# Cross-attention, attention and expert kernel: expert chunks stored and loaded one tile earlier, turned rows for two value projections from a second area, two buffers for finished values

## The chip, the cores and the metric

The kernel runs on one core of a Trainium2 chip. The metric is the device time of one execution in microseconds (us). The median of three runs of the kernel before is 1504.02 us (1499.2 to 1504.85).

## What is computed

Two layers in float32 over x of 8 batches, 512 tokens and 512 features, each behind a layer norm and added to its input. The first is a cross-attention in which every token looks at itself and at 77 context rows. The second adds a self-attention with 16 heads and a mixture of 8 experts, two of them per token.

```python
def xattn(h, ctx):                       # h = layernorm(x)
    q, k_tok, v_tok = h @ Wq + bq, h @ Wk + bk, h @ Wv + bv
    k_ext, v_ext = ctx @ Wk + bk, ctx @ Wv + bv
    scores = concat([sum(q * k_tok, -1)[..., None], einsum('bsh,beh->bse', q, k_ext)], -1)
    p = softmax(scores)
    return p[..., :1] * v_tok + einsum('bse,beh->bsh', p[..., 1:], v_ext)

def ffn(h):                              # h = layernorm(x1)
    q, k, v = split(h @ W_qkv + b_qkv)   # 16 heads of 32
    attn_out = softmax(q @ k.T / sqrt(32)) @ v
    top_g, top_i = top_k(softmax(h @ W_gate + b_gate), 2)
    moe_out = sum over the 2 chosen experts of g * (h @ W_experts[e] + b_experts[e])
    return attn_out + moe_out

x1 = x + xattn(layernorm(x), ctx)
out = x1 + ffn(layernorm(x1))
```

## The kernel before

Five programs, one for each engine queue, are written by hand and meet at semaphores; no scheduler moves anything. TensorE (PE) multiplies, VectorE (DVE), ScalarE (ACT) and GpSimd (POOL) do the elementwise work, and SyncE (SP) issues nearly all DMAs, in the order of its program. A wait in SP's program holds everything that is written behind it. Every operand of a large product is kept as a high and a low part, so that one product is three matmuls (`prod3`, lines 222 to 224).

The program has four stages.

- **Setup** (to about 118 us) prepares the folded weights.
- **Tile stage** (about 118 to 450 us). 32 tiles of 128 tokens (`NT` = 32, four in a batch, `T` = 4) go through the cross-attention, the second norm and the gate. Each engine has a `steps(b, part)` that lists its work of one tile step with an offset: ACT's step i does `p_hi` of tile i-1 (L704), `chunk_hi` of chunk i (L698), `weigh` of tile i (the softmax's exponential, L709), `h_hi` of i+1, `h_norm` of i+2, `h2_hi` of i-2, and `h2_norm` of tile i-1 (L660). DVE's step i begins with `p_lo` of i-1 (L1251), and has `largest` of i (to L1274), `x1_whole` of i-1 (L1280), `share` of i (L1286, L1288), `h2_stats`, `h_lo` (L1245) and at its end `chunk_lo` (L1303). PE's step ends with `p_turn` of tile i (L947), which needs `share`. POOL computes the two norms' factors (L516 to L522). Beside the tiles, each step splits one chunk of the expert weights (128 x 512, 32 chunks in all) into a high and a low part: SP loads it to one of two staging buffers `raw` (`load_chunk`, L358), ACT and DVE write the parts to one of two buffers `chunk`, and SP stores them (`store_chunk`, L362).
- **Attention stage** (about 487 to 1222 us). 8 batches of 16 heads. While batch b's heads run, the dense products of the later heads (items R0 to R3) and of batch b+1 (V0 to V3 for values, N0 to N3 for queries and keys) are cut in halves and laid between them by the tables `HALVES` and `STEP`: R3 at head 4, V0 begins at head 5, V1 ends at head 7, V2 begins at head 13. All products read the turned rows of the batch, `fT`, four tiles of 128 x 1024, which SP fetches from DRAM (`fetch_turned`, L355) once R3 is done with the previous contents. `V` is copied from `Vst` by a DMA at the batch's start (L441). The `L415` DMAs stack query and key rows. DVE's `finish` divides a pair of heads by its sums and writes it to `tmp` (L1567); after four pairs POOL adds `tmp` to the output in DRAM (`attended`, L548), twice in a batch (h = 0 and 1). The first pair of each half waits until the addition before has landed (`f_att_out`).
- **Expert stage** (to the end). 72 blocks of 128 chosen rows are gathered (L590), turned, multiplied with an expert and added to the output (L601).

Of the kernel before, what the change touches and what calls it, by code (L numbers as in the profile page):

```python
# [6 lines left out]
ALU = mybir.AluOpType  # L7
# [8 lines left out]
def program(nc, x, ctx, wq, bq, wk, bk, wv, bv, w_qkv, b_qkv, w_gate, b_gate, w_exp, b_exp, out):  # L16
# [15 lines left out]
    C = D // P  # L32
# [12 lines left out]
    with ExitStack() as stack:  # L45
# [26 lines left out]
        def full(part):  # L72
            return part.bitcast(F32)
# [54 lines left out]
        fT = (fT_all[:, :, 0], fT_all[:, :, 1])  # L128
        fT_in = full(area(parts, 6 * C * D, T, 2 * D))
        NSLOT = 5  # L130
        SLOTS = (r0, r0 + 4 * S, r4, r4 + 4 * S, r4 + 8 * S)
# [15 lines left out]
        Osb = area(plain, p1, QW)  # L147
        tmp = area(plain, p1 + S, T, D // 2)
        bvf = sb("bias_v_all", [P, D])
# [46 lines left out]
        p2 += NE * D  # L196
        rows = [area(plain, p2 + D * i, D) for i in range(4)]
        ysb = [area(plain, p2 + D * (4 + i), D) for i in range(4)]
        col = sb("col", [P, 2, 4])
# [9 lines left out]
        in_list in_be r_ranked ws_in0 ws_in1 ws_hi ws_lo ws_out0 ws_out1 m_ready in_ew0 in_ew1 in_ew2 in_ew3 in_ew4 in_ew5 in_ew6 in_ew7 m_rows0 m_rows1  # L209
        m_rows2 m_rows3 m_tr m_hi m_hT m_full m_sum m_y m_added0 m_added1 m_added2 m_added3 m_done f_att_out x1_out0 x1_out1 x1_out2 x1_out3  # L210
        h2_out0 h2_out1 h2T_out0 h2T_out1 h2T_out2 h2T_out3 made_gate made_steps""".split()
# [124 lines left out]
        def _(sp):  # L336
# [28 lines left out]
            def tiles(b, more, first=False):  # L365
                for t in range(T):
                    if t or not first:
                        store_chunk(b + (t - 1) // T, (t - 1) % T)
                    if t and (more or t < T - 1):
                        load_chunk(b + (t + 1) // T, (t + 1) % T)  # L370
                    elif not first and t == 0:
                        load_chunk(b, 1)
                    if not more and t == 2:

                        sp.wait_ge(q["v_full"], NT)
                        for u in range(T):
                            sp.wait_ge(q[f"h2T_out{u}"], 16)
                        fetch_turned(0)
                    if more:

                        sp.wait_ge(q["x1_part"], b * T + t + 1)
                        sp.dma_start(xin[:, t, :], x_t[b * T + t + T]).then_inc(q[f"x_in{t}"], 16)
                    sp.wait_ge(q["x1_ready"], b * T + t + 1)
                    sp.dma_start(out_t[b * T + t], x1[:, t, :]).then_inc(q[f"x1_out{t}"], 16)
                    sp.wait_ge(q["h2_ready"], b * T + t + 1)
                    sp.dma_start(h2_t[b * T + t], h2[:, t % 2, :]).then_inc(q[f"h2_out{t % 2}"], 16)
                    if t or not first:
                        turned_out(b * T + t - 1, t + T - 1)
# [7 lines left out]
            tiles(B - 1, False)  # L396
            store_chunk(NE - 1, C - 1)
            turned_out(NT - 1, T - 1)
# [29 lines left out]
            def load_expert(r):  # L428
# [6 lines left out]
                sp.dma_start(ew[r], ws_dram[bass.ds(e, 1)].rearrange("e p n -> p (e n)")).then_inc(q[f"in_ew{r}"], 16)  # L435

            def batch(b, first, last):
                sp.wait_ge(q["f_d_free"], number(b, "R0")[0])
                sp.sem_inc(q["sp_went_on"], 1)
                await_ge(sp, "f_pv", 2 * b * NQ)  # L440
# [49 lines left out]
        def _(pool):  # L490
# [53 lines left out]
            def attended(b, h):  # L544

                pool.wait_ge(q["f_o_fin"], b * NQ + 4 * h + 4)
                pool.sem_inc(q["pool_went_on"], 1)
                pool.dma_start(out_b[b][:, :, h * (D // 2):(h + 1) * (D // 2)], tmp, accum_op=ALU.add).then_inc(q["f_att_out"], 16)  # L548

# [59 lines left out]

            pool.wait_ge(q["f_att_out"], 16 * 2 * B)  # L610
            for i in range(NB):
# [228 lines left out]
        def _(pe):  # L840
# [146 lines left out]
            def dense(b, item, n, o, half=""):  # L987
                kind, t = item[0], int(item[1])
                cs = {"": range(C), "a": range(C // 2), "b": range(C // 2, C)}[half]
                if kind == "V":  # L990
                    if half != "b":
                        pe.wait_ge(q[f"f_in{t}"], b * 16 + 16)
                    for c in cs:
                        last = prod3(pe, o[:], at(fT, sl, t, c), at(wV, sl, c), c == 0, c == C - 1)
                else:
# [172 lines left out]
        def _(dve):  # L1168
# [326 lines left out]

            big = area(plain, 3 * C * D + T * D + NT * NE, NB, NE)
            other = area(plain, 3 * C * D + T * D + NT * NE + NB * NE, NB, NE)

# [57 lines left out]
            def finish(b, p):  # L1556
# [6 lines left out]
                if p % HG == 0:  # L1563
                    await_ge(dve, "f_att_out", (2 * b + p // HG) * 16)
                for m in range(2):
                    at_d = m * P + p % HG * HD
                    ins = dve.tensor_tensor(  # L1567
                        tmp[:, :, at_d:at_d + HD].rearrange("p (x t) d -> p t x d", x=2),
                        bank[6][:, 0:QW].rearrange("p (t m x d) -> p m t x d", t=2, m=2, x=2)[:, m],
# [38 lines left out]
            def blocks(n, part):  # L1608
                for k in range(U):
# [6 lines left out]

                    await_ge(dve, "m_done", i - 3)
                    dve.tensor_tensor(ysb[k % 4], bank[2 + k % 2][:], be_all[:, bass.ds(e * D, D)], ALU.add).then_inc(q["m_sum"], 1)  # L1618

# [33 lines left out]
```

## Time and profile before

| | |
|---|---|
| runs | 1499.2, 1504.02, 1504.85 us; median 1504.02 |
| profiled execution | 1503.07 us, of which the span (first to last instruction) is 1501.4 us |
| PE | 1351.7 us busy, 90% of the span; mean granted clock 0.935 |
| DVE | 968.8 us, 65% |
| ACT | 902.2 us, 60% |
| POOL | 358.6 us, 24% |
| SP's DMA queue | 166.13 MB, 37.3% of the 16 DMA engines' time |
| POOL's DMA queue | 42.04 MB, 16.5% |

An engine's busy share is an average over stages with different limits, so the stages are read apart. PE's matmuls are pipelined and their ends are modelled. A wait is put down to the releaser that came last. In a line of the timeline the number in brackets is the idle time of the engine before that instruction and the arrow names what ended it. The granted clock is a share of full speed.

### The profile page before, as it was taken

What the parts mean: (1) busy time and instruction counts of PE and PEld (TensorE: products, weight loads), DVE (VectorE), ACT (ScalarE), POOL (GpSimd) and SP (SyncE); (2) the same over time, 40 slices, a digit from 0 to 9 for tenths busy, and PEclk for the clock granted to TensorE, in tenths of its full rate; (3) what the DMA queues carried; (4) which work ended last, traced back from release to release, by engine and by line L of the source; (5) the groups of instructions that cost most, each with busy time, mean ns of one, the idle gap of its engine ahead of it and who ended that gap; (6) DMA issues with size and microseconds to landing.
All of it is one profiled execution on the core that took longest, in us unless ns stands there. A gap on an engine that the chain in (4) does not pass through costs nothing. (4 is left out here: it accounts for less than half of the span.)

```text
span 1501.4 us, 27639 instructions
## 1 busy us (share of the span) xinstructions
PE 1351.7 (90%) x7744; PEld 1028.0 (68%) x7745; DVE 968.8 (65%) x2143; ACT 902.2 (60%) x1888; POOL 358.6 (24%) x572
## 2 busy tenths in 40 slices
PE   4989989898988889999999999999997769999997
PEld 4957777776777556676676767667774437777775
DVE  4246666666666888787887878888885633433332
ACT  4123333333334778899999989999996753333332
POOL 0001112121110001121211112120001007777765
PEclk9998887989899999999999999999997779999998
DMA  5014555555557523646445474544567757877873
GB/s 153 1 58 161 201 191 194 197 197 194 200 180 221 148 58 94 155 99 159 86 100 136 107 154 98 141 91 111 132 115 185 278 196 137 145 130 126 146 128 57
DMA packets 111371, 212.49 MB, mean 142 GB/s; under 512 B 28265, under 2 KB 36585, under 8 KB 109139
## 3 DMA queue, kind: packets, MB, share of 16 engines
q1 hardware_dynamic: 82048, 166.13, 37.3%
q0 software_dynamic: 26624, 42.04, 16.5%
q10 hardware_dynamic: 2643, 3.65, 0.8%
q8 instruction: 27, 0.44, 0.1%
q14 instruction: 29, 0.24, 0.1%
HBM read 79.48 MB, written 77.73 MB: 105 GB/s over the span
## 5 line engine op out<-in xcount | busy, mean ns | idle before, releaser
L222 PE MATMUL banks<-parts 128*128 128x512 f32 (+6 forms) x1108 | 453.8, 410 | 57.4 <-DVE parts L1245 19.6
L224 PE MATMUL banks<-parts 128*128 128x512 f32 (+6 forms) x1108 | 432.0, 390 | 0.0
L223 PE MATMUL banks<-parts 128*128 128x512 f32 (+6 forms) x1108 | 431.7, 390 | 0.0
L1538 DVE TENSOR_REDUCE plain<-banks 128x1 f32<-128x512 f32 x512 | 339.6, 687 | 95.6 <-PE banks L1042 89.6
L766 ACT ACTIVATE banks<-banks,plain 128x512 f32<-128x512 f32 x512 | 345.0, 678 | 14.9 <-DVE plain L1538 14.6
L773 ACT ACTIVATE plain<-banks 128x1024 f32<-128x1024 f32 x256 | 265.7, 1038 | 60.5 <-PE banks L1064 58.9
L222 PEld LDWEIGHTS banks<-parts 128*128 128x128 f32 (+1 forms) x1108 | 220.8, 199 | 114.9 <-issue 46.9
L224 PEld LDWEIGHTS banks<-parts 128*128 128x128 f32 (+1 forms) x1108 | 219.8, 198 | 41.7
L223 PEld LDWEIGHTS banks<-parts 128*128 128x128 f32 (+1 forms) x1108 | 221.4, 200 | 30.6
L1042 PE MATMUL banks<-parts 96*128 96x512 f32 x512 | 186.5, 417 | 0.7 <-ACT banks L766 0.3
L1064 PE MATMUL banks<-parts 104*128 104x512 f32 x512 | 180.7, 435 | 6.0 <-ACT plain L773 4.6
L548 POOL DMA_DIRECT2D out_dram<-plain x16 | 22.2, 1390 | 575.0 <-DVE plain L1567 490.8
L816 ACT CAST parts<-banks 128x512 fp32r<-128x512 f32 x72 | 42.1, 586 | 170.6 <-PE banks L1140 170.6
L1618 DVE TENSOR_TENSOR plain<-banks,plain 128x512 f32<-128x512 f32 x72 | 49.8, 692 | 142.5 <-PE banks L224 127.5
L1083 PE MATMUL banks<-plain,parts 128*32 128x256 f32 x2048 | 132.2, 401 | 0.2 <-ACT plain L773 0.2
L698 ACT CAST parts<-plain 128x512 fp32r<-128x512 f32 x32 | 19.9, 620 | 181.5 <-DMA plain<-in_L_ffn_W_experts_dram 181.5
L601 POOL DMA_INDIRECT out_dram<-plain,score_bias x72 | 114.0, 1583 | 53.0 <-issue 24.6
L1042 PEld LDWEIGHTS banks<-parts 96*128 96x128 f32 x512 | 99.3, 195 | 38.6 <-issue 8.8
L766 ACT ACTIVATION_READ_ACCUMULATOR banks<-banks,plain 128x1 f32 x512 | 115.1, 225 | 0.0
L1064 PEld LDWEIGHTS banks<-parts 104*128 104x128 f32 x512 | 86.6, 196 | 33.2 <-issue 15.0
L1083 PEld LDWEIGHTS banks<-plain,parts 128*32 128x32 f32 x2048 | 62.2, 114 | 63.3 <-issue 32.1
L516 POOL TENSOR_TENSOR mo<-mo,consts 128x1 f32<-128x1 f32 x64 | 12.1, 190 | 377.8 <-DVE mo L1236 377.8
(180 smaller groups left out, 1602.0 us busy)
## 6 DMA issues: line engine op xcount, KB each, us to landing
parts<-parts SPq DMA_DIRECT2D x384, 128.0 KB, 2.4
experts_split<-parts SPq DMA_DIRECT2D x32, 512.0 KB, 4.3
h_turned<-parts SPq DMA_DIRECT2D x32, 512.0 KB, 2.9
parts<-h_turned SPq DMA_DIRECT2D x32, 512.0 KB, 6.8
parts<-experts_split SPq DMA_DIRECT2D x8, 2048.0 KB, 11.5
plain<-in_x_dram SPq DMA_DIRECT2D x32, 256.0 KB, 4.2
plain<-in_L_ffn_W_experts_dram SPq DMA_DIRECT2D x32, 256.0 KB, 4.3
out_dram<-plain SPq DMA_DIRECT2D x32, 256.0 KB, 2.6
```

The costliest lines, as they stand in the source:

```text
L222: pe.matmul(out, stat[0], mov[0], start=first, stop=False)
L223: pe.matmul(out, stat[0], mov[1], start=False, stop=False)
L224: return pe.matmul(out, stat[1], mov[0], start=False, stop=last)
L601: pool.indirect_dma_start(out=out_rows, out_offset=bass.IndirectOffsetOnAxis(ap=lst[:, i, 0:1].bitcast(U32), axis=0), in_=ysb[i % 4], in_o ...
L766: act.activation(bank[SB[t]][:], bank[SB[t]][:], ACT.Exp, bias=nmx[:, k, t:t + 1], accum_out=Z[:, t, k:k + 1]).then_inc(q["f_exp"], 1)
L773: act.activation(PT[k % HG][:, c:c + 2, :], banks[0][:], ACT.Exp).then_inc(q["f_pt"], 1)
L816: act.copy(gT[k][:, 0].rearrange("p c n -> p (c n)"), bank[k][:]).then_inc(q["m_hi"], 1)
L1042: pe.matmul(bank[SB[t]][:], stk[slot][0][0:M0, m, t * P:(t + 1) * P], stk[slot][1][0:M0, m, :], start=True, stop=True).then_inc(q["f_s_ful ...
L1064: pe.matmul(bank[c % 2][:], stk[slot][1][0:M1, m, c * P:(c + 1) * P], stk[slot][0][0:M1, m, :], start=True, stop=True).then_inc(q["f_t_ful ...
L1083: last = pe.matmul(bank[6][o * HD:(o + 1) * HD, 0:QW], V[:, c, head * HD:(head + 1) * HD], PT[(2 * p + m) % HG][:, c, x * QW:(x + 1) * QW] ...
L1538: dve.tensor_reduce(nmx[:, k, t:t + 1], bank[SB[t]][:], AX.X, ALU.max, negate=True).then_inc(q["f_max"], 1)
L1618: dve.tensor_tensor(ysb[k % 4], bank[2 + k % 2][:], be_all[:, bass.ds(e * D, D)], ALU.add).then_inc(q["m_sum"], 1)
```

## The change

Four edits, and some areas of on-chip memory that move.

1. **Chunks.** In SP's tile step t, `store_chunk` now takes the chunk of this tile where it took the one of the tile before, and `load_chunk` fetches the chunk of tile t+2 where it fetched that of t+1. ACT's and DVE's steps are as before.
2. **Turned rows for V0 and V1.** A new area `fU` of two tiles is filled by SP at the start of each batch but the last (`fetch_ahead`). The halves of V0 and V1 that are laid between heads read `fU`; V2, V3 and N0 to N3 read `fT`. `fetch_turned` still fetches all four tiles. The first `fetch_ahead` waits for the stored expert chunks, since `fU` lies over one of their buffers.
3. **Finished values.** `tmp` has two buffers, one for each half of a batch, and `f_att_out` becomes two semaphores. `finish` waits for the addition of the same half of the batch before.
4. **Areas.** `rows` and `ysb` of the expert stage and two temporaries of the routing move. Two of the `ysb` buffers lie over the new `tmp`, so DVE's first block waits for `f_att_out0`.

```diff
+        fU_in = full(area(parts, r4 + 12 * S, 2, 2 * D))
+        fU_all = area(parts, r4 + 12 * S, 2, 2 * D).rearrange("p t (a c n) -> p t a c n", a=2, c=C)
+        fU = (fU_all[:, :, 0], fU_all[:, :, 1])
...
-        tmp = area(plain, p1 + S, T, D // 2)
+        tmp = (area(plain, HG * T * S + D, T, D // 2), area(plain, p1 + S, T, D // 2))
...
-        rows = [area(plain, p2 + D * i, D) for i in range(4)]
-        ysb = [area(plain, p2 + D * (4 + i), D) for i in range(4)]
+        rows = [area(plain, p2 + D * i, D) for i in (0, 3, 4, 5)]
+        ysb = [area(plain, p2 + D * i, D) for i in (6, 7, 1, 2)]
...
             def tiles(b, more, first=False):
                 for t in range(T):
-                    if t or not first:
-                        store_chunk(b + (t - 1) // T, (t - 1) % T)
-                    if t and (more or t < T - 1):
-                        load_chunk(b + (t + 1) // T, (t + 1) % T)
-                    elif not first and t == 0:
-                        load_chunk(b, 1)
+                    store_chunk(b, t)
+                    if more or t < T - 2:
+                        load_chunk(b + (t + 2) // T, (t + 2) % T)
...
+            def fetch_ahead(b):
+                for t in range(2):
+                    sp.dma_start(fU_in[:, t], ft_dram[b * T + t]).then_inc(q[f"f_u{t}"], 16)
+
             def batch(b, first, last):
                 sp.wait_ge(q["f_d_free"], number(b, "R0")[0])
+                if first:
+                    sp.wait_ge(q["ws_out0"], 16 * NE * C // 2)
+                if not last:
+                    fetch_ahead(b + 1)
...
-                pool.dma_start(out_b[b][...], tmp, accum_op=ALU.add).then_inc(q["f_att_out"], 16)
+                pool.dma_start(out_b[b][...], tmp[h], accum_op=ALU.add).then_inc(q[f"f_att_out{h}"], 16)
...
                 if kind == "V":
-                    if half != "b":
+                    ahead = half != "" and t < 2
+                    if ahead and half == "a":
+                        pe.wait_ge(q[f"f_u{t}"], b * 16)
+                    elif half != "b":
                         pe.wait_ge(q[f"f_in{t}"], b * 16 + 16)
                     for c in cs:
-                        last = prod3(pe, o[:], at(fT, sl, t, c), at(wV, sl, c), c == 0, c == C - 1)
+                        last = prod3(pe, o[:], at(fU if ahead else fT, sl, t, c), at(wV, sl, c), c == 0, c == C - 1)
...
                 if p % HG == 0:
-                    await_ge(dve, "f_att_out", (2 * b + p // HG) * 16)
+                    await_ge(dve, f"f_att_out{p // HG}", b * 16)
...
+                    if part == "first" and k == 0:
+                        dve.wait_ge(q["f_att_out0"], 16 * B)
```

The diff moves instructions of SP alone. The first place is SP's loop of the tile stage, where its first tile step ends and its second begins. `experts_split` is the store of a chunk, `in_L_ffn_W_experts_dram` a load, `h_turned` the store of turned rows. Before:

```order
L386 DMA h_rows<-plain 128x512 [waits h2_ready]
L351 ISA [waits h2T_ready]
L351 DMA h_turned<-parts 128x1024
L362 ISA [waits ws_lo]
L362 DMA experts_split<-parts 256x1x512
L358 ISA
L358 DMA plain<-in_L_ffn_W_experts_dram 128x512
L381 REGISTER_ALU
L382 ISA [waits x1_part]
L382 DMA plain<-in_x_dram 128x512
```

Now:

```order
L386 DMA h_rows<-plain 128x512 [waits h2_ready]
L354 ISA [waits h2T_ready]
L354 DMA h_turned<-parts 128x1024
L364 REGISTER_ALU
L365 ISA [waits ws_lo]
L365 DMA experts_split<-parts 256x1x512
L361 ISA
L361 DMA plain<-in_L_ffn_W_experts_dram 128x512
L382 ISA [waits x1_part]
L382 DMA plain<-in_x_dram 128x512
```

The row order is the same; what differs is the number waited for in `ws_lo` and the chunk that is loaded, each one further on.

The second place is SP's queue at the start of the first attention batch, up to the fetch of the turned rows. Before:

```order
L415 DMA parts<-parts 32x2x512 x5
L441 DMA parts<-plain 128x2048 [waits f_d_free]
L415 DMA parts<-parts 32x2x512 [waits f_d_free,f_t_full]
L415 DMA parts<-parts 32x2x512 x5
L355 DMA parts<-h_turned 128x1024 [waits f_d_full]
L355 DMA parts<-h_turned 128x1024 x3
```

Now:

```order
L414 DMA parts<-parts 32x2x512 x5
L438 DMA parts<-h_turned 128x1024 [waits ws_out0,f_d_free]
L438 DMA parts<-h_turned 128x1024
L448 DMA parts<-plain 128x2048
L414 DMA parts<-parts 32x2x512 [waits f_d_free,f_t_full]
L414 DMA parts<-parts 32x2x512 x5
L358 DMA parts<-h_turned 128x1024 [waits f_d_full]
L358 DMA parts<-h_turned 128x1024 x3
```

Two loads of turned rows stand ahead of the copy of V; the four behind them stay.

## Rows read from the trace of the kernel before

**Rows 1.** The page, 40 equal slices of 37.5 us: granted TensorE clock in tenths.

```profile
PEclk9998887989899999999999999999997779999998
```

**Rows 2.** Windows: stretch, length, busy time (count) of PE, PEld, DVE, ACT, POOL, clock.

```profile
150.00:300.00 150.00, 133.55 (x695) 112.50 (x694) 96.68 (x284) 51.91 (x119) 28.00 (x109) 0.86 0.56 196
700.00:1000.00 300.00, 290.44 (x1896) 207.51 (x1896) 241.76 (x502) 275.72 (x597) 52.40 (x80) 0.99 0.51 120
```

**Rows 3.** Waits from 150 to 450 us: engine, line, releaser, us in total, times, longest.

```profile
ACT parts L698 <- DMA plain<-in_L_ffn_W_experts_dram: 162.4, 28, 7.2
...
PE banks L222 <- DVE parts L1245: 16.5, 17, 1.2
PE banks L947 <- DVE sc L1288: 13.7, 12, 2.2
```

**Rows 4.** Timeline, one tile step on SP and ACT: start, duration, instruction.

```profile
229.04 0.48 SPq L358 DMA_DIRECT2D plain<-in_L_ffn_W_experts_dram  x1
...
239.90 0.55 SPq L358 DMA_DIRECT2D plain<-in_L_ffn_W_experts_dram  x1
...
233.53 0.62 ACT L698 CAST parts<-plain 128x512 fp32r<-128x512 f32 x1 [6.33 <-DMA plain<-in_L_ffn_W_experts_dram]
...
237.23 0.82 ACT L660 ACTIVATE plain<-plain,mo 128x512 f32<-128x512 f32 x1 [1.08 <-POOL mo L522]
```

**Rows 5.** Line 947, the turn of the shares, once a tile; durations in ns.

```profile
L947 PE MATMUL banks<-ident,sc x32: 270/274/284, 120.4 to 448.6; 128*78 128x128 f32 x32
```

**Rows 6.** Timeline of PE: two pairs of neighbours.

```profile
173.42 0.28 PE L947 MATMUL banks<-ident,sc 128*78 128x128 f32 x1
...
181.59 0.27 PE L947 MATMUL banks<-ident,sc 128*78 128x128 f32 x1
...
224.13 0.28 PE L947 MATMUL banks<-ident,sc 128*78 128x128 f32 x1 [1.19 <-DVE sc L1288]
225.59 0.47 PE L222 MATMUL banks<-parts 128*128 128x512 f32 x1 [1.18 <-DVE parts L1245]
```

**Rows 7.** Windows of the tile stage: a step at full clock, and the stretch behind it.

```profile
214.00:222.00 8.00, 7.63 (x50) 6.56 (x49) 5.62 (x16) 1.16 (x3) 2.03 (x8) 1.00 0.63 210
225.00:235.00 10.00, 9.41 (x38) 8.37 (x39) 6.12 (x18) 2.84 (x9) 1.99 (x8) 0.59 0.61 210
```

**Rows 8.** Timeline of ACT and DVE around one step's border.

```profile
204.67 0.82 ACT L660 ACTIVATE plain<-plain,mo 128x512 f32<-128x512 f32 x1 [0.81 <-POOL mo L522]
206.42 0.26 ACT L704 CAST parts<-banks 78x128 fp32r<-78x128 f32 x1 [0.94 <-PE banks L947]
...
201.99 0.16 DVE L1286 RECIPROCAL col<-col 128x1 f32<-128x1 f32 x1 [0.96 <-ACT sc L709]
...
210.20 0.68 DVE L1280 TENSOR_TENSOR plain<-banks,plain 128x512 f32<-128x512 f32 x1
```

**Rows 9.** Waits of PE's weight loads for turned rows, 480 to 1222 us.

```profile
PEld banks L222 <- DMA parts<-h_turned: 10.6, 5, 3.3
```

**Rows 10.** Timeline of POOL: the second addition of batches 0, 5 and 6.

```profile
599.71 1.40 POOL L548 DMA_DIRECT2D out_dram<-plain  x1 [6.78 <-DVE plain L1567]
...
1041.43 1.40 POOL L548 DMA_DIRECT2D out_dram<-plain  x1 [25.59 <-DVE plain L1567]
...
1127.27 1.28 POOL L548 DMA_DIRECT2D out_dram<-plain  x1 [42.13 <-issue]
```

**Rows 11.** Batch 3: the copy of V is issued, and PE's first load that uses it.

```profile
767.37 0.53 SPq L441 DMA_DIRECT2D parts<-plain  x1
...
778.55 0.37 PEld L1083 LDWEIGHTS banks<-plain,parts 128*32 128x32 f32 x12 [0.36 <-issue]
```

**Rows 12.** Issue to landing, us, shortest, median, longest: line 355's fetches, then line 548's additions.

```profile
DMA to landing us min/median/max: 3.4/6.8/11.2
...
DMA to landing us min/median/max: 7.4/8.0/14.3
```

**Rows 13.** Timeline of DVE in batch 7: the finished values' first pair.

```profile
1141.71 0.49 DVE L1567 TENSOR_TENSOR plain<-banks,plain 128x128 f32<-128x128 f32 x2 [6.67 <-DMA out_dram<-plain]
```

More of the change, by code:

```diff
@@ L209, in program @@
         in_list in_be r_ranked ws_in0 ws_in1 ws_hi ws_lo ws_out0 ws_out1 m_ready in_ew0 in_ew1 in_ew2 in_ew3 in_ew4 in_ew5 in_ew6 in_ew7 m_rows0 m_rows1
-        m_rows2 m_rows3 m_tr m_hi m_hT m_full m_sum m_y m_added0 m_added1 m_added2 m_added3 m_done f_att_out x1_out0 x1_out1 x1_out2 x1_out3
+        m_rows2 m_rows3 m_tr m_hi m_hT m_full m_sum m_y m_added0 m_added1 m_added2 m_added3 m_done f_att_out0 f_att_out1 f_u0 f_u1 x1_out0 x1_out1 x1_out2 x1_out3
         h2_out0 h2_out1 h2T_out0 h2T_out1 h2T_out2 h2T_out3 made_gate made_steps""".split()
@@ L396, in _ @@
             tiles(B - 1, False)
-            store_chunk(NE - 1, C - 1)
             turned_out(NT - 1, T - 1)
@@ L547, in attended @@
                 pool.sem_inc(q["pool_went_on"], 1)
-                pool.dma_start(out_b[b][:, :, h * (D // 2):(h + 1) * (D // 2)], tmp, accum_op=ALU.add).then_inc(q["f_att_out"], 16)
+                pool.dma_start(out_b[b][:, :, h * (D // 2):(h + 1) * (D // 2)], tmp[h], accum_op=ALU.add).then_inc(q[f"f_att_out{h}"], 16)
             for t in range(T):
@@ L608, in _ @@
             attended(B - 1, 1)
-            pool.wait_ge(q["f_att_out"], 16 * 2 * B)
+            for h in range(2):
+                pool.wait_ge(q[f"f_att_out{h}"], 16 * B)
             for i in range(NB):
@@ L1494, in second_records @@
                 choice_records(1)
-            big = area(plain, 3 * C * D + T * D + NT * NE, NB, NE)
-            other = area(plain, 3 * C * D + T * D + NT * NE + NB * NE, NB, NE)
+            big = area(plain, 3 * C * D + T * D + 4 * NT * NE + D, NB, NE)
+            other = area(plain, 3 * C * D + T * D + 4 * NT * NE + D + NB * NE, NB, NE)
             def block_experts():
@@ L1567, in finish @@
                     ins = dve.tensor_tensor(
-                        tmp[:, :, at_d:at_d + HD].rearrange("p (x t) d -> p t x d", x=2),
+                        tmp[p // HG][:, :, at_d:at_d + HD].rearrange("p (x t) d -> p t x d", x=2),
                         bank[6][:, 0:QW].rearrange("p (t m x d) -> p m t x d", t=2, m=2, x=2)[:, m],
```

## The prediction

> **What bounds the kernel now.** I read the slices of the page first, then windows, then the waits of each window, then the timeline of single steps. The slices show three regions: a clock of 7 to 9 tenths in slices 4 to 12 (the tile stage), 9 tenths or more up to slice 30 (attention), and 7 tenths in slices 31 to 33 (the end of attention) [rows 1]. In the tile stage PE is busy 133.55 of 150 us at a mean granted clock of 0.86; in the middle of the attention stage 290.44 of 300 us at 0.99 [rows 2]. So attention is bound by PE, with little to win, while the tile stage has both idle PE and a slower clock.
>
> Who holds the tile stage? ACT waits 162.4 us, in 28 of 28 tiles, for the load of the expert chunk [rows 3]. ACT is not the busy engine (51.91 of 150 us, [rows 2]), so this costs only if it closes a circle, and it does. SP issues a chunk's load at 229.04; ACT takes the chunk at 233.53, 4.49 later; only behind it stand the softmax's exponential and the rest of ACT's step, whose last piece `h2_norm` ends at 237.23 + 0.82 = 238.05, 4.52 later; SP, whose program has the store of that row ahead of the next chunk, issues the next load at 239.90, 1.85 later [rows 4]. The sum is 10.86 us. The stage's own period: the turn of the shares runs from 120.4 to 448.6 in 31 steps [rows 5], 328.2 / 31 = 10.59 us. They agree: the tile stage runs at the pace of a circle that goes through a load issued one tile too late. All other engines fit themselves into it.
>
> **Part 1, the chunks.** The load of chunk t+2 now goes out at the place in SP's queue where that of t+1 went. Nothing is added: as many loads and stores, in the same order. SP's new wait is for the chunk that DVE has just split at the end of the step, ahead of DVE's `x1_begun`, for which SP waits next anyway; behind it are the x load and three stores, all of which wait for later pieces of DVE's program. So the wait holds nobody, and I cost it at nothing; if that cover were gone, x rows for three tiles on would be late. A load then has one whole step more than its 4.49 us, so ACT's wait of about 5.8 us (162.4 / 28) goes and the circle is open.
>
> What is late next? (a) PE. Its quickest step at full clock, without a wait, took 181.59 - 173.42 = 8.17 us [rows 6]; the mean busy time of a step is 133.55 x 10.59 / 150 = 9.43 us at clock 0.86 [rows 2], and 9.43 x 0.86 = 8.1 at full clock. Steps with the gate's products are longer than those without, so I take 8.5, the upper side. (b) The circle of ACT, DVE and POOL that stays: from `p_hi` (206.42) to the end of `x1_whole` (210.20 + 0.68 = 210.88) 4.46 us, and from `share` (201.99, the step before) to the end of `h2_norm` (204.67 + 0.82 = 205.49) 3.50 us [rows 8]; behind it `p_hi` can start again: 7.96 us. DVE alone is busy 96.68 x 10.59 / 150 = 6.8 us in a step [rows 2]. So PE binds by a small margin, at 8.5 us. The gain is (10.59 - 8.5) x 31 = **65 us**. Its bounds: at 8.1 us it is 77, and if the clock stays at 0.86 a step cannot be under 9.43, which leaves (10.59 - 9.43) x 31 = 36.
>
> **The clock** decides between these. PE waited 1.19 and 1.18 us at 224.13 and 225.59 [rows 6]; in the 8 us before the granted clock was 1.00, in the 10 us behind it 0.59, mostly the 1.2 GHz level [rows 7]. In the attention stage, with PE 97% busy, it is 0.99 [rows 2]. The tile stage's falls stand behind such gaps, and the gaps are waits for `share` and `h_lo` (13.7 and 16.5 us in [rows 3]), both of which come late because ACT waited for the chunk. With them gone I take the clock to stay at 2.4 GHz nearly throughout. The Trainium skill, "TensorE: Matmul & The Clock Gate", section "A second HAM failure mode: psum-queue depth-cycling", says that short idle spots between groups of matmuls, if frequent, are enough to make the clock swing. By that rule the clock would still swing in a step that keeps some tenths of idle time, and the gain would be the 36 us above; this trace speaks against it, as the step from 214 to 222 us kept 0.37 us idle at 1.00 [rows 7].
>
> **Part 2, turned rows ahead.** PE waited 10.6 us in five batches for the first value tile's fetch [rows 9]. `fU` is filled from the batch's start, five heads ahead, so the wait goes. What it cost in all is seen in the period: from batch 0's second addition to batch 5's 441.72 us, 88.34 for a batch, against 1127.27 - 1041.43 = 85.84 for batch 6, which had no wait [rows 10]: 5 x 2.5 = 12.5 us. That is more than 10.6, since the clock fell behind the longest wait. I take **13**; bounds 9 (ACT, busy 275.72 of 300 us, becomes the bound for a part) and 16 (the sixth batch's addition was itself issued a little late). It adds 14 fetches of 512 KB. They stand ahead of the copy of V and of the stacks for the second half. The copy of V is issued 11.2 us before PE first needs it [rows 11], and SP reaches the new fetches before it, since the copy also waits for the last products with the old V. A fetch lands in 3.4 to 11.2 us [rows 12]. I cost them at 0, at most 3 us a batch where V is pushed past its 11.2. The Trainium skill, "DMA: Bandwidth & Descriptors", section "Queues, rings and completion order", says that each DMA engine takes the descriptors of one ring in their order, so 1 MB put ahead of V must delay it by its own length if both are pending at once. By that the cost would be up to the 3 us above; no row here shows such a pair.
>
> **Part 3, two buffers.** Of 16 additions one was waited for: batch 7's first pair of finished values stood 6.67 us for the addition issued at 1127.27 [rows 13, 10], which took 14.3 us to land where the median is 8.0 [rows 12]. It now writes the other buffer, whose addition went out half a batch earlier. PE stood too, and slices 31 to 33 show a lower clock behind it [rows 1]. I take **7**; bounds 5 and 10. The extra wait of DVE's first expert block is for an addition issued some 40 us before, so it costs 0. The moved areas change no instruction: 0.
>
> **Sum.** 65 + 13 + 7 = 85 us off the profiled execution's 1503.07: 1418.07. That execution is 0.95 below the median of the runs (1504.02), so the forecast is **1418** us, 5.7% less.
>
> **Rivals.**
> - *The clock keeps swinging in the tile stage.* 36 + 13 + 7 = 56: 1447. For it: PE's margin over the circle of 7.96 is small, so waits remain; against it: [rows 7]. 0.15.
> - *Another circle binds at 9.2 us.* The circle of 7.96 passes four engines, and each landing or queue that slips adds to it; x rows must land one and a half steps ahead, with traffic denser by 10.59 / 8.5. The gain is 1.39 x 31 = 43: 43 + 20 = 63, 1440. 0.12.
> - *The change doesn't do what it says*: SP reaches the loads so late that ACT still waits, the tile stage keeps its pace and only parts 2 and 3 pay: 20 us, 1483. Against it: SP's place in the queue is unchanged and the chunk is needed a step later. 0.03.
> - *Slower.* The 1 MB ahead of V in seven batches delays V and the stacks, PE stands in each, and the clock falls. To lose 85 + 7.5 us it must cost 13 us in each batch, so V would land 24 us after its issue. The worst landings are 11.2 and 14.3 [rows 12]; the latter would cost 3.1 us a batch, 22 in all. Below 24 us this does not decide. 0.02.
> - *More than forecast*: steps of 8.1 us and all upper bounds, 77 + 16 + 10 = 103: 1400. 0.04.
>
> **How the numbers follow.** The forecast has 0.64; its own range is 1404 to 1432. The range from 1400 to 1456 takes in the two rivals at 1440 and 1447 with the cost of 3 us a batch on part of the batches, and holds some 0.9. A difference of about 0.5% (7.5 us) is what a measurement of this kernel can tell from no change. Only the fourth rival is slower; no change would need it to cost as much as the three parts give. Faster 0.96, same 0.02, slower 0.02.
>
> **What the profile after would show.** Right: no wait of ACT for chunks, line 947's 31 steps in some 263 us, PEclk 9 or full in the tile stage's slices, PE's idle time there under 0.5 us a step; no wait for the turned rows at heads 5 to 7 and batches of 85 to 86 us; no wait of DVE for an addition in batch 7. Wrong: steps of 9.4 us with PE busy at 0.86 (the clock), steps of 9 us and more with PE idle before `p_turn` or the next score (another circle, named by the releaser), ACT's wait kept, or PE waiting for V at head 3. The sum would be most wrong if the clock's falls have a cause other than PE's gaps.

## The result, and the profile after

The changed kernel takes 1406.47 us (median of four runs, 1402.42 to 1412.21), the kernel before in the same comparison 1502.62. The ratio is 0.9365, with an interval of 0.9322 to 0.9407: 6.4% less, where 5.7% was forecast (1418, range 1400 to 1456). The profiled execution of after took 1412.21 us with a span of 1410.6, against 1501.4.

The page of after, the slices of 35.3 us each, PE's busy share above and the granted clock below, to be laid beside [rows 1]:

```profile
PE   4998999999888899999999999999988779999996
PEclk9998999999899999999999999999996789999998
```

Inside the tile stage (now slices 5 to 10) the clock reads 9 throughout, and 8 in the two slices at its borders (4 and 11), where [rows 1] had 8 in five slices and 7 in one; slices 31 to 33 are as low as before. A window of 200 us in the tile stage (columns as in [rows 2]), and one of the attention stage:

```profile
130.00:330.00 200.00, 199.47 (x1234) 172.37 (x1232) 172.73 (x512) 95.20 (x212) 53.17 (x200) 1.00 0.74 259
...
700.00:900.00 200.00, 198.00 (x1321) 142.19 (x1321) 167.67 (x349) 189.71 (x412) 38.70 (x59) 1.00 0.60 143
```

PE is busy 199.47 of 200 us at full clock, against 133.55 of 150 at 0.86. It is now what bounds the tile stage. The turn of the shares, which answers to [rows 5] (line 947 is line 955 now), and the costliest waits from 130 to 380 us, which answer to [rows 3]:

```profile
L955 PE MATMUL banks<-ident,sc x32: 270/270/272, 120.7 to 371.8; 128*78 128x128 f32 x32
```

```profile
POOL mo L523 <- DVE mo L1247: 176.6, 59, 6.8
ACT sc L717 <- DVE col L1285: 93.3, 30, 4.1
ACT plain L668 <- POOL mo L529: 32.9, 30, 2.0
DVE parts L1262 <- ACT parts L712: 23.8, 29, 1.2
...
PE banks L225 <- DVE parts L1262: 2.6, 2, 1.4
```

31 steps take 371.8 - 120.7 = 251.1 us, 8.10 a step, where they took 328.2, 10.59 a step. ACT's wait of 162.4 us for the chunks has left the list; ACT now waits for DVE instead, which costs nothing, since PE waits 2.6 us for line 1262 and 0.5 us for line 1256 in the whole stretch.

One thing is new. The timeline of PE behind the last tile, then two windows there:

```profile
380.92 0.76 PE L225 MATMUL banks<-parts 128*128 128x512 f32 x1 [5.41 <-DMA parts<-h_turned]
```

```profile
372.00:382.00 10.00, 3.41 (x19) 2.63 (x19) 5.88 (x8) 4.22 (x6) 4.62 (x7) 0.84 0.88 299
382.00:392.00 10.00, 10.00 (x41) 7.95 (x40) 2.27 (x4) 3.30 (x5) 0.00 (x0) 0.82 0.45 174
```

PE stands 5.41 us for the first fetch of turned rows (line 358), and in the 10 us behind it the clock is 0.82. Before the change PE waited 0.50 us for this fetch, but it also had a wait for DVE at this border, which is 1.2 us now:

```profile
452.18 0.77 PE L222 MATMUL banks<-parts 78*128 78x512 f32 x1 [3.30 <-DVE parts L1251]
```

POOL's additions cut the attention stage, as in [rows 10] (line 548 is line 555 now): the second ones of batches 0, 6 and 7.

```profile
526.29 1.41 POOL L555 DMA_DIRECT2D out_dram<-plain  x1 [6.95 <-DVE plain L1578]
...
1039.75 1.28 POOL L555 DMA_DIRECT2D out_dram<-plain  x1 [42.06 <-issue]
...
1132.08 1.30 POOL L555 DMA_DIRECT2D out_dram<-plain  x1 [41.86 <-PE banks L1151]
```

By such marks the profiled spans divide as follows (us; the difference of the spans is -90.8):

| stretch | before | after | difference |
|---|---|---|---|
| start to the first turn of shares | 120.4 | 120.7 | +0.3 |
| 31 tile steps | 328.2 | 251.1 | -77.1 |
| last turn of shares to batch 0's second addition | 151.1 | 154.5 | +3.4 |
| batches 1 to 6 | 527.6 | 513.5 | -14.1 |
| batch 7 | 95.9 | 92.3 | -3.6 |
| to the end | 278.2 | 278.5 | +0.3 |

### The profile page after: what moved, and what is told of

It is laid out like the page before. It is cut to its first block and busy times, and to the rows that moved or that the text cites. A ratio compares the mean times of both kernels' runs of the same rounds, so it can differ in the third digit from the quotient of the medians.

```text
span 1410.6 us, 27655 instructions
## 1 busy us (share of the span) xinstructions
PE 1305.5 (93%) x7744; PEld 994.7 (71%) x7745; DVE 967.5 (69%) x2143; ACT 903.4 (64%) x1888; POOL 363.8 (26%) x572
## 5 line engine op out<-in xcount | busy, mean ns | idle before, releaser
L225 PE MATMUL banks<-parts 128*128 128x512 f32 (+6 forms) x1108 | 443.0, 400 | 32.7 <-DVE parts L1334 7.4
L227 PE MATMUL banks<-parts 128*128 128x512 f32 (+6 forms) x1108 | 423.5, 382 | 0.0
L226 PE MATMUL banks<-parts 128*128 128x512 f32 (+6 forms) x1108 | 422.9, 382 | 0.0
L225 PEld LDWEIGHTS banks<-parts 128*128 128x128 f32 (+1 forms) x1108 | 214.2, 193 | 85.4 <-issue 24.2
L227 PEld LDWEIGHTS banks<-parts 128*128 128x128 f32 (+1 forms) x1108 | 213.0, 192 | 40.8
L226 PEld LDWEIGHTS banks<-parts 128*128 128x128 f32 (+1 forms) x1108 | 214.4, 194 | 30.8
L1563 DVE TENSOR_TENSOR parts<-banks,plain 8x512 fp32r<-8x512 f32 x128 | 89.2, 697 | 21.5 <-PE banks L1064 18.0
```

Source lines behind the costliest of these rows:

```text
L225: pe.matmul(out, stat[0], mov[0], start=first, stop=False)
L226: pe.matmul(out, stat[0], mov[1], start=False, stop=False)
L227: return pe.matmul(out, stat[1], mov[0], start=False, stop=last)
L1563: dve.tensor_tensor(stk[slot][0][M0:M1, m, :].rearrange("p (t n) -> p t n", t=T), bank[6][M0:M1, 0:P].unsqueeze(1).broadcast_to([2 * T, T, ...
```

## The experiments

The first three do one part of the change each, without the others.

**The chunks alone**: edit 1.

```diff
-                    if t or not first:
-                        store_chunk(b + (t - 1) // T, (t - 1) % T)
...
+                    store_chunk(b, t)
+                    if more or t < T - 2:
+                        load_chunk(b + (t + 2) // T, (t + 2) % T)
```

> The kernel before with part 1 alone: each tile step stores its own chunk and loads the chunk two on. Theory (the tile stage ran at the pace of a circle through a load issued one tile too late; opened, PE sets the pace at its full clock): line of the turned shares at 8.1 us a step as in the changed kernel, against 10.59; 77 us less in the tile stage, of which 3 to 5 us come back where PE waits for the fetch of the first turned rows; in all 1502.6 - 73 = about 1430 us, and the clock full through the tile stage. Rival (the three parts need each other, for instance the clock stays up only together): steps of 8.5 us or more and over 1445 us.

1425.31 against 1504.57 us, ratio 0.9474 (0.946 to 0.9488): -79.3 us. The row of its turn of the shares:

```profile
L943 PE MATMUL banks<-ident,sc x32: 270/270/272, 119.4 to 369.0; 128*78 128x128 f32 x32
```

That is 249.6 / 31 = 8.05 us a step. Part 1 alone gives the full pace of the tile stage, and also the late fetch: PE waits 5.5 us there too, so that wait belongs to part 1 and not to the added fetches. In the attention stage PE's and its weight loads' waits for turned rows stay (8.6 and 10.8 us), and DVE still waits 6.4 us for an addition in batch 7.

**The second area of turned rows alone**: edit 2.

```diff
+            def fetch_ahead(b):
+                for t in range(2):
+                    sp.dma_start(fU_in[:, t], ft_dram[b * T + t]).then_inc(q[f"f_u{t}"], 16)
```

> The kernel before with part 2 alone: V0 and V1 read turned rows fetched a batch ahead. Theory: the five waits (10.6 us) go, and the clock's falls behind them; batches 1 to 5 take 85.5 us each as in the changed kernel (441.7 before, 427.8 after): 14 us less, about 1489 us, ratio 0.991. Rival (the wait was covered by ACT, busy 92% of the attention stage, and the batch got shorter for another reason, such as the two buffers): 5 us less or nothing, ratio 0.997 or more.

1491.47 us, ratio 0.9913 (0.9898 to 0.9927): -13.1 us. Its additions that end batches 0 and 5:

```profile
606.02 1.40 POOL L559 DMA_DIRECT2D out_dram<-plain  x1 [6.89 <-DVE plain L1581]
...
1033.99 1.40 POOL L559 DMA_DIRECT2D out_dram<-plain  x1 [25.59 <-DVE plain L1581]
```

Five batches take 427.97 us, 85.6 each, where they took 88.34. In the kernel after it is 427.76. No wait for turned rows is left in its attention stage. The mechanism of part 2 holds, and its size.

**Two buffers for finished values alone**: edit 3 and the areas it needs.

```diff
-                    await_ge(dve, "f_att_out", (2 * b + p // HG) * 16)
+                    await_ge(dve, f"f_att_out{p // HG}", b * 16)
```

> The kernel before with part 3 alone: finished values have two buffers. Theory (the 6.67 us wait stood in front of a second stall of the same place, in which ACT, DVE and PE all wait for some 2.5 us while a 2 MB expert load fills the DMA engines; so only the rest is won): batch 7 takes 92.3 us from the second addition of batch 6 to its own, against 95.9 before; 3 to 4 us less in all, ratio 0.9975. Rival (all of the 6.67 us is won and the changed kernel lost half of it by its other parts): 7 us less, ratio 0.9955.

1497.53 us, ratio 0.9949 (0.9934 to 0.9964): -7.0 us. Batch 7 in its profile:

```profile
1129.97 1.28 POOL L548 DMA_DIRECT2D out_dram<-plain  x1 [41.99 <-issue]
...
1217.07 1.30 POOL L548 DMA_DIRECT2D out_dram<-plain  x1 [41.84 <-PE banks L1141]
```

87.10 us, against 95.89 before. After seeing only 3.6 us of gain in batch 7 of the kernel after, I had expected about that here; that expectation fell, and the 7 us of the prediction stood. The medians carry this, with an interval of 5.4 to 9.9 us, and not the single profile: with its wait for the addition still there, batch 7 took 96.41 us with the chunks alone and 92.64 with the turned rows alone.

**The changed kernel again**, on the chip of these three, to see whether the parts add up.

> The changed kernel once more, on the same chip as the three parts. If the parts add up, its gain is the sum of the three gains within their intervals (73 + 14 + 4 = 91 us); if one part needs another, it is larger than the sum by 5 us or more; if they take from each other, smaller.

1406.2 us, ratio 0.9333 (0.9313 to 0.9353): -98.4 us. The parts alone sum to 79.3 + 13.1 + 7.0 = 99.4. They are additive within the measurement: part 1 works in the tile stage, parts 2 and 3 at different places of the attention stage, and no profile shows one of them opening another's wait. Its batch 7 took 86.19 us (1040.69 to 1126.88), not 92.33, so the small gain of batch 7 in the first profile was that execution's and not the change's. Executions differ in other places too: here the stretch behind batch 7 took 285.0 us, against 278.5.

**Is it the load's time that held the tile stage?** If the circle through the chunk's load set the pace, a longer load must lengthen the step of the kernel before, and leave the kernel after alone. Ahead of each chunk's load another load of 256 KB goes into an area that nobody reads:

```diff
             def load_chunk(e, c):
+                await_ge(sp, f"x_extra{c % 2}", 32 * e + 16 * (c // 2))
+                sp.dma_start(spare[:, c % 2], w_exp[...]).then_inc(q[f"x_extra{c % 2}"], 16)
```

In the kernel before:

> The kernel before with one more 256 KB load (of the same chunk, to an unused place) issued by SP just ahead of each chunk load. It leaves nothing out. Theory (the pace of the tile stage is the circle load - ACT - SP): the chunk's load is issued some 0.6 us later and lands behind 256 KB more, so the 10.59 us of a step grow by that delay, 1.2 to 2 us; 37 to 62 us in all, and ACT's wait for the load stays. Rival (the pace was set by PE with its slow clock, and ACT's wait was only idle time): steps as before, under 0.3 us longer.

1529.3 against 1498.08 us, ratio 1.0209 (1.0173 to 1.0245): +31.2. Its waits and its window from 150 to 450 us:

```profile
ACT parts L703 <- DMA plain<-in_L_ffn_W_experts_dram: 174.6, 25, 7.9
```

```profile
150.00:450.00 300.00, 258.69 (x1280) 218.62 (x1279) 180.63 (x519) 96.36 (x218) 52.27 (x202) 0.82 0.58 201
```

In the kernel after:

> The changed kernel with the same extra load ahead of each chunk load. Theory: a load now has a whole step more than it needs, so the delay is hidden and the tile stage keeps 8.1 us a step at full clock, although it moves 2.3 MB a step instead of 2.05; under 5 us in all. Rival (the DMA queue is close to its limit at 259 GB/s, so denser traffic pushes x rows or chunks past their need): steps of 8.5 us or more, with ACT or DVE waiting for a DMA.

1404.23 us, ratio 0.9374 (0.9341 to 0.9407), as without the extra loads:

```profile
130.00:330.00 200.00, 199.47 (x1234) 172.54 (x1233) 173.16 (x511) 95.20 (x212) 52.56 (x200) 1.00 0.85 293
```

The same bytes cost the kernel before 1.01 us a step (turns from 119.8 to 479.5, 11.60 us a step) and the kernel after nothing, though its DMA engines are now busy 85% of the time. The step of before did hang on the load; the expected 1.2 to 2 us was somewhat too much. The traffic itself, half as dense again as in [rows 2] (293 against 196 GB/s), isn't a limit here, and no engine waits for a DMA in the 31 steps. That also answers the concern of the second rival, that x rows land late when traffic grows.

**How far behind PE is the next circle?** In the kernel after one more DVE instruction stands at the head of `h2_stats`, inside the circle of ACT, DVE and POOL; it writes to an unused column.

```diff
+                dve.tensor_reduce(fence[:, 2:4], sbias[:, 0:600].unsqueeze(1).broadcast_to([P, 2, 600]), AX.X, ALU.max)
```

> The changed kernel with one more instruction of DVE in each tile step, ahead of the second norm's statistics: a maximum over 2 x 600 values, some 1.3 us, whose result is used nowhere. It measures the prediction's next circle (7.96 us, ACT - DVE - POOL) and the clock. Theory: that circle grows to 7.96 + 1.3 = 9.3 us and takes over from PE (8.1), so steps are 9.3 us with PE idle 1.2 us in each; the clock, whose falls followed gaps of over 2 us before, stays full or nearly so, and the kernel is 36 us slower than the changed one. Rival on the clock (short idle spots, if frequent, make it swing): it falls in several steps, as before, and steps are longer than 9.3. Rival on the circle (DVE has more room than the circle says): steps under 8.8 us.

1436.54 us, ratio 0.959 (0.9556 to 0.9624). The added instruction, the turns, and the window from 150 to 350 us:

```profile
L1302 DVE TENSOR_REDUCE fence<-score_bias 128x2 f32<-128x1200 f32 x23 | 32.1, 1396 | 0.0
```

```profile
L955 PE MATMUL banks<-ident,sc x32: 270/270/272, 119.4 to 399.8; 128*78 128x128 f32 x32
```

```profile
150.00:350.00 200.00, 187.29 (x1123) 157.68 (x1123) 181.96 (x481) 83.18 (x191) 45.58 (x178) 0.99 0.66 234
```

A step takes 280.4 / 31 = 9.05 us. Without the 1.40 us added the circle would be at 7.65. Line 712 of ACT (`p_hi`) starts right behind `h2_norm` in the timeline of ACT:

```profile
255.23 0.81 ACT L668 ACTIVATE plain<-plain,mo 128x512 f32<-128x512 f32 x1 [2.38 <-POOL mo L529]
255.95 0.24 ACT L712 CAST parts<-banks 78x128 fp32r<-78x128 f32 x1
```

DVE is busy 181.96 of 200 us, so its own work alone doesn't fill the step. It is the circle that the prediction named under (b), with a size of 7.65 where 7.96 was read from two single steps. PE's 8.10 lies 0.45 above it. The run with four times 600 elements, below, gives the same size: 10.27 - 2.65 = 7.62. The clock stays at 0.99, though PE now waits in nearly every step (20 waits for line 1256's parts, 12.7 us in all, the longest 0.7).

**How large must PE's waits be before the clock falls?** The same instruction over four and six times 600 elements, to make the waits longer.

> As the kernel with one more instruction of DVE in each tile step, but over 4 x 600 values, 2.7 us; its result is used nowhere. The shorter one (1.40 us) gave steps of 9.05 us, so the circle without it is some 7.7 us. Theory: it grows linearly, to 7.7 + 2.6 = 10.3 us a step, nearly the 10.59 us of the kernel before; PE is then idle 2.2 us a step in one or two places, as in the kernel before, and if gaps of that size are what lets the clock fall, it falls in the tile stage again (mean 0.85 to 0.95), without making the steps longer, since DVE sets the pace. Rival (the falls before had another cause than the gaps): a clock of 0.98 or more at the same idle time. In all 76 us more than the changed kernel.

1474.16 us, ratio 0.9832 (0.9795 to 0.9868).

> The same over 6 x 600 values, 3.9 us. Theory: 11.6 us a step, PE idle 3.5 us in each, the clock at 0.80 to 0.90 in the tile stage; steps follow the circle alone. Rival: a clock of 0.98 or more, or steps longer than 12 us because PE at half clock joins the circle.

1526.77 us, ratio 1.0182 (1.0141 to 1.0224). The added instructions take 2.65 and 3.90 us. The turns run from 121.2 to 439.7 with four, 10.27 us a step, and from 120.5 to 491.6 with six, 11.97 us. The timeline of PE with four more, two neighbouring steps:

```profile
285.10 0.27 PE L955 MATMUL banks<-ident,sc 128*78 128x128 f32 x1
287.28 0.47 PE L225 MATMUL banks<-parts 128*128 128x512 f32 x1 [1.91 <-DVE parts L1256]
...
295.18 0.27 PE L955 MATMUL banks<-ident,sc 128*78 128x128 f32 x1
297.43 0.47 PE L225 MATMUL banks<-parts 128*128 128x512 f32 x1 [1.98 <-DVE parts L1256]
```

Its window over 16 such steps:

```profile
250.00:410.00 160.00, 129.97 (x781) 109.02 (x779) 148.34 (x339) 58.17 (x133) 33.07 (x128) 1.00 0.59 207
```

With six more, a wait and the windows in front of it and behind it:

```profile
191.95 0.47 PE L225 MATMUL banks<-parts 128*128 128x512 f32 x1 [2.81 <-DVE parts L1256]
```

```profile
180.00:189.00 9.00, 9.00 (x57) 7.60 (x55) 8.32 (x19) 3.85 (x9) 1.94 (x8) 1.00 0.66 233
192.00:200.00 8.00, 8.00 (x33) 7.12 (x34) 6.39 (x17) 3.09 (x7) 1.36 (x6) 0.56 0.68 243
```

The step with four more is nearly as slow as that of the kernel before (10.27 against 10.59) and PE stands still for 30 of 160 us, but at full clock: its 16 waits lie between 1.7 and 2.0 us. With six more, eight of the 11 waits from 150 to 350 us are 2.8 to 3.2 us, and behind 2.81 us the clock falls from 1.00 to 0.56; in that stretch it is 0.82 on average, much as in the kernel before with its extra loads (0.83). The steps came out at 11.97 us, longer than the 11.6 expected: without the added instruction that is 8.07, which the circle of 7.65 alone does not account for. With four more the clock also fell before 250 us, most in three windows of 10 us (0.66, 0.69 and 0.74), each with one wait in it: 1.53, 1.91 and 1.91 us. A wait of 1.91 us at 287.28 and one of 1.98 us at 297.43 left it at 1.00. So waits of about 1.9 us went either way in this kernel, and the changed kernel has a fall behind a shorter one, the only wait of its tile steps above 0.5 us, with the clock in the window behind it 0.51:

```profile
349.35 0.47 PE L225 MATMUL banks<-parts 78*128 78x512 f32 x1 [1.40 <-DVE parts L1262]
```

```profile
351.50:355.00 3.50, 3.50 (x12) 2.82 (x11) 3.36 (x12) 2.11 (x5) 1.10 (x5) 0.51 0.20 75
```

The two waits of [rows 6], 1.19 and 1.18 us, stand 0.28 us apart and come to 2.37 us together. The falls read here all stand behind waits; which waits bring one about, these runs don't settle. The Trainium skill, "TensorE: Matmul & The Clock Gate", section "A second HAM failure mode: psum-queue depth-cycling", describes a kernel in which frequent short idle spots between groups of matmuls made the clock swing; in the 160 us above, some 16 steps with a wait of 1.7 to 2.0 us in each, it didn't.

**The expert weights' load later.** In the first profile of after, PE, ACT and DVE all stood still around 1044 to 1047 us, in batch 7, beside transfers that filled the DMA engines. The first expert's weights are loaded in that stretch; here they are asked for behind the heads.

```diff
-                    load_expert(0)
...
+                    load_expert(0)
                     load_expert(1)
```

> The changed kernel with the first 2 MB expert load of the last batch issued some 40 us later, with the second one. Theory (in the changed kernel's profile ACT, DVE and PE stood together for 2.3 to 3.3 us early in batch 7, while the DMA engines were busy 99% with that load, and a stack load issued behind it held SP for 6 us): the stop goes, batch 7 takes 85 to 87 us in every profile, and the median falls by 1 to 4 us. Rival (the stop has another cause, or the loads after it are late for the expert stage): no change, or the expert stage begins later, up to 8 us slower.

1406.71 us, ratio 0.9395 (0.937 to 0.9419); batch 7 took 86.16 us, as it does in other executions with the load in its place. It gains nothing: its ratio to the kernel before is no better than those of the changed kernel (0.9333 to 0.9365 in three comparisons). A shorter stop of ACT, during which PE stands 1.5 us, is still there, 6.0 us behind the second addition of batch 6 (6.7 us in the first profile), with the DMA engines 72% busy in the 15 us from that addition on:

```profile
1042.27 0.37 ACT L786 COPY plain<-banks 128x256 f32<-128x256 f32 x1 [2.11 <-remote]
```

So a stop of this kind comes without the expert load beside it.

**The first fetch of turned rows in halves**, to shorten the 5.4 us that PE stands behind the last tile. N0 and N1 of the first batch begin with the first half of the features.

```diff
-                        fetch_turned(0)
+                        for g in range(2):
+                            for u in range(T):
...
+                                sp.dma_start(halved[:, u][:, :, cs], src[:, :, cs]).then_inc(q[f"f_in{u}" if g else "f_h0"], 16)
```

> The changed kernel with the first fetch of turned rows (2 MB, for which PE waited 5.4 to 6.0 us) cut in two: first the upper half of the features of all four tiles, then the lower half; PE works through the first half of N0 and N1 between the two. Theory: PE starts after 1 MB, some 4 us sooner, stands a second time for 1 to 2 us, and the clock stays full behind it: 2 to 5 us less, ratio to the changed kernel 0.997 to 0.9985. Rival (pieces of 1 KB in place of 4 KB land more slowly than the cut wins): no change or 1 to 3 us slower.

1402.97 us, ratio 0.9356 (0.9331 to 0.938). Beside it, on the same chip, the changed kernel:

> The changed kernel on the same chip, for comparison with the fetch in halves. Its batch 7 tells how often the stop is there that its first profile showed (92.3 us against 86.2 in the second).

1402.2 us, ratio 0.9351 (0.9326 to 0.9376). The timeline with halves, of SP and of PE:

```profile
373.59 5.21 SPq L383 DMA_DIRECT2D parts<-h_turned  x8
```

```profile
380.35 0.58 PE L225 MATMUL banks<-parts 128*128 128x512 f32 x1 [3.22 <-issue]
```

PE's wait shrinks from 5.4 to 3.2 us, the clock from 382 to 392 us is 0.90 where it was 0.82, and the stretch from the last turn to batch 0's second addition from 154.7 to 152.8. The 1.9 us do not show in the medians, which differ by 0.8 the other way, inside their intervals. SP needs 5.21 us to issue the eight halves, where the four whole fetches took 1.77. No version here beats the changed kernel measurably.

## Why the prediction was right, and where it was off

- **The bound of before.** The reading that the tile stage ran at the pace of a circle through a chunk's load stands: part 1 alone took ACT's wait away and the step from 10.59 to 8.05 us, and an extra load ahead of the chunk's lengthened the step before the change and not behind it.
- **The term of part 1, 65 us, was mis-sized**: it measured 79.3 alone, and 77.1 in the tile steps. The step of the working that failed is the choice of 8.5 us as the "upper side" of PE's step. The reason for it, that steps with the gate's products are longer than those without, doesn't raise the mean over the 8.1 us that the same paragraph worked out as busy time at full clock (9.43 x 0.86). 8.1 was a mean over 14 steps, so the longer steps were in it already. PE took 8.10. The gain came out at the bound that the text gave, 77.
- **The clock** came out as argued: [rows 7] was the right row. With PE's waits gone it is 1.00 in the window of 200 us, with one short fall behind a wait of 1.40 us. The first rival (1447, clock swinging on) fell: even waits of 0.5 to 0.7 us in nearly every step left the clock at 0.99. The prediction did not say what size of wait matters, and the runs with four and six more give no plain limit.
- **The next circle** was named rightly and read 0.3 us too long (7.96 against 7.65). The second rival (1440, another circle at 9.2) fell; one more DVE instruction of 1.40 us makes such a case, 9.05 us a step.
- **"Costs nothing" of the chunk's moved wait** held in the tile stage. What I had not asked is what the faster stage would collide with behind it: at the last tile PE reaches the first batch's products before the turned rows are fetched, waits 5.41 us (0.50 us for this fetch before the change), and the clock falls to 0.82 behind it. The stretch grew by 3.4 us, which is less than the wait, since a wait of 3.30 us for DVE stood at this border before.
- **Part 2, 13 us**: 13.1 alone. The working from the periods (88.34 against 85.84) was right, and batches of 85 to 86 us came. What the added fetches do to the copy of V is seen in its eight landings, in the kernel before and then in the kernel after:

```profile
DMA to landing us min/median/max: 4.5/4.6/5.7
```

```profile
DMA to landing us min/median/max: 4.5/4.6/7.4
```

  In the first batch the copy goes out 1.1 us behind the two fetches (413.25 and 414.38) and lands after 7.4 us, where the first batch's took 4.6 before; the longest landing is 7.7 and 7.2 us in the two repeated runs of the changed kernel. In the other batches SP issues the fetches 7.8 to 8.6 us ahead of the copy (680.34 and 688.82 in batch 3) and it lands in 4.5 to 4.8 us. The Trainium skill, "DMA: Bandwidth & Descriptors", section "Queues, rings and completion order", has each DMA engine take one ring's descriptors in their order; the trace agrees in the one batch where the two are pending together, a delay of 2.8 us, and the rule has nothing to act on in the others. The fourth rival (slower) fell all the same: nobody waits for V, which PE first uses at 430.74 in the first batch, 16 us after the copy was issued.
- **Part 3, 7 us**: 7.0 alone. DVE's wait for the addition went, and PE's longest wait behind it fell from 6.5 to 1.4 us. The lower clock that the prediction saw behind this wait did not go with it: over batch 7 it was 0.75 before, 0.76 with part 3 alone and 0.76 in the profile of after.
- **The sum.** 65 + 13 + 7 = 85 was forecast; 79.3 + 13.1 + 7.0 = 99.4 measured part by part, 98.4 together, 96.2 in the first comparison. The error is part 1's, and it has the sign of caution: a bound computed from many steps was passed over for a rounded-up one.

What stays open is batch 7. It took 92.33 us in the profile of after and 91.08 with two more on DVE, but 84.8 to 88.0 in seven other profiles with all three parts. In the long one ACT, DVE and PE stand at once:

```profile
1046.48 0.37 ACT L786 COPY plain<-banks 128x256 f32<-128x256 f32 x1 [2.83 <-remote]
1046.52 1.29 DVE L1549 TENSOR_REDUCE plain<-banks 128x1 f32<-128x512 f32 x2 [3.27 <-remote]
...
1047.00 0.28 PE L1064 MATMUL banks<-ident,neg_max_parts 128*104 128x128 f32 x1 [2.26 <-issue]
```

```profile
1039.75:1055.00 15.25, 12.99 (x93) 8.90 (x95) 9.63 (x21) 11.04 (x25) 5.46 (x5) 0.89 0.99 291
```

The DMA share there is 0.99, but it is 1.02 in the same stretch of the repeated run, which took 86.19 us. Shorter stops of about 2 us are there in batches of 86 and 88 us as well. Full DMA engines alone don't explain it, and the expert load isn't shown to cause it, since a shorter stop came without it; the cause stays open.

## What to carry to other kernels

When an idle engine waits in every step for the same load, add up the circle from the load's issue over its consumer to what the issuing queue waits for; if the sum is the step's period, asking for the load one step sooner is worth the whole distance to the next bound, and here the clock came back with it, from 0.86 to 1.00. Take that next bound from the busy time of many steps at full clock, not from a rounded single step, and look for the second circle close behind it. Where a stage becomes faster, read its border to the next one: here a transfer that the old pace had hidden stood open there.

## What the runs showed of the hardware that I had not expected

- The granted clock bore much more waiting than I had thought: some 16 steps in a row with PE standing 1.7 to 2.0 us in each, 30 us of 160, ran at 1.00. With six more, most waits 2.8 to 3.2 us, it swung between 1.00 and about 0.5 and was 0.82 on average. The sum of the waits didn't tell the two apart: from 150 to 350 us PE stood 31.4 us with four more, at a mean clock of 0.95, and 29.9 us with six more, at 0.82. The length of the single wait isn't the whole answer either: the kernel before stood 21.7 us in that stretch, no wait over 2.2 us, at 0.85, and in the changed kernel the clock fell behind 1.40 us. What decides stays open.
- Three engines can stand still at once for 2 to 3 us, with no releaser on the core that the profile shows, in some executions and not in others of the same kernel, while the transfers go on.
- Traffic of 293 GB/s with the DMA engines 85% busy did not slow the tile stage of the changed kernel: 8.06 us a step (250.0 / 31), against 8.10 without the extra loads. In the kernel before, where a load had no step in hand, the same extra bytes cost 1.01 us a step.
